# A three-part layer kernel whose first halves start from other counts and take their later loads piece by piece

## The reference

```python
x = x + attn_a(layernorm(x))   # delta-rule attention: per token S = a*S@(I - b k k^T) + b v k^T, o = (q@S)*gate, then @ Wo + bo
x = x + ffn(layernorm(x))      # silu(x @ gate^T) * (x @ up^T) @ down^T, int weights / 127
x = x + attn_b(layernorm(x))   # Mamba-like: causal convolution, chunked state space, gate, RMS norm, @ W_out
x = x + ffn(layernorm(x))
```

## Time and profile before

| | |
|---|---|
| median of three runs | 869.94 us (869.21 to 869.99) |
| profiled execution, first to last instruction (span) | 868.0 us |
| instructions | 16041 |
| TensorE busy | 769.9 us, 89% |
| VectorE (DVE) busy | 614.7 us, 71% |
| ScalarE (ACT) busy | 535.9 us, 62% |
| GpSimd (POOL) busy | 560.6 us, 65% |
| DMA | 22.16 MB, of it 11.59 MB read from HBM |

### The profile page before, as it was taken

How to read it: one execution, slowest core, us unless ns; L and a number is a source line. 1 busy time by engine, 2 the same in 40 slices (tenths; PEclk the granted TensorE clock), 3 DMA queues, 4 the chain that set the end, 5 groups by cost and what they waited for, 6 DMA issues and landing times. The chain is left out here.

```text
span 868.0 us, 16041 instructions
## 1 busy us (share of the span) xinstructions
PE 769.9 (89%) x5114; PEld 549.0 (63%) x5114; DVE 614.7 (71%) x1739; ACT 535.9 (62%) x1035; POOL 560.6 (65%) x917
## 2 busy tenths in 40 slices
PE   1469999999999896999848899999999999959997
PEld 1368888888888673666625466565555555646665
DVE  1356788788788544888673878988887776638885
ACT  2224443444454234899645888888887787818886
POOL 1276676677667512877711689779778876757785
PEclk9979999999999898999855999999999999979999
DMA  7511111211111100000000000000000000000112
GB/s 192 141 28 42 43 28 35 49 29 28 45 40 29 28 14 1 0 1 0 2 1 8 1 1 5 5 1 1 9 2 1 7 3 2 2 0 26 48 49 74
DMA packets 59420, 22.16 MB, mean 26 GB/s; under 512 B 22224, under 2 KB 59088, under 8 KB 59344
## 3 DMA queue, kind: packets, MB, share of 16 engines
q1 hardware_dynamic: 59344, 21.23, 9.6%
HBM read 11.59 MB, written 9.63 MB: 24 GB/s over the span
## 5 line engine op out<-in xcount | busy, mean ns | idle before, releaser
L1411 DVE SCALAR_TENSOR_TENSOR arena<-bank,convw_sb,arena 128x510 f32<-128x510 f32 (+2 forms) x192 | 142.5, 745 | 41.7 <-ACT arena L902 37.0
L671 POOL TENSOR_TENSOR arena<-arena 128x768 f32<-128x768 f32 x64 | 114.8, 1815 | 10.5 <-ACT arena L929 10.5
L645 POOL TENSOR_TENSOR arena<-ff,arena 128x512 f16<-128x512 f32 x64 | 73.6, 1159 | 23.2 <-ACT arena L871 21.2
L866 ACT ACTIVATE ff<-bank 128x512 f32<-128x512 f32 x96 | 56.2, 586 | 32.7 <-PE bank L1716 32.5
L578 POOL TENSOR_TENSOR leafV<-leafV,leaf_tmp 32x14 f32<-32x14 f32 (+6 forms) x224 | 62.1, 277 | 17.5
L1803 PE MATMUL bank<-xnT,win_sb 128*128 128x512 f32 x128 | 71.8, 644 | 0.0
L1227 DVE SCALAR_TENSOR_TENSOR ff<-bank,ff 128x512 f32<-128x512 f32 x96 | 64.7, 685 | 9.5 <-ACT ff L866 8.8
L759 ACT ACTIVATE xnT<-bank 128x512 f32<-128x512 f32 x34 | 20.3, 596 | 81.0 <-PE bank L1542 81.0
L767 ACT ACTIVATE xn<-x_all,shift,rstd 128x128 f32<-128x128 f32 x136 | 55.6, 481 | 23.7 <-DVE shift L1032 23.6
L774 ACT ACTIVATE ff<-bank 128x256 f32<-128x256 f32 (+2 forms) x80 | 33.9, 424 | 58.0 <-PE bank L1555 36.0
L923 ACT ACTIVATE arena<-bank 128x384 f32<-128x384 f32 x128 | 59.8, 491 | 13.8 <-PE bank L1818 13.6
(11 more groups left out here) (202 smaller groups left out, 2233.4 us busy)
## 6 DMA issues: line engine op xcount, KB each, us to landing
LT_dram<-arena SPq DMA_DIRECT2D x16, 256.0 KB, 2.3
ff<-R_dram SPq DMA_DIRECT2D x16, 256.0 KB, 2.8
out<-x_all SPq DMA_DIRECT2D x8, 512.0 KB, 3.2
x_all<-in_L_attn_a_x SPq DMA_DIRECT2D x7, 512.0 KB, 7.2
ff<-pieces_dram SPq DMA_DIRECT2D x48, 6.0 KB
x_all<-in_L_attn_a_x SPq DMA_DIRECT2D x2, 256.0 KB, 3.7
R_dram<-tab SPq DMA_DIRECT2D x2, 256.0 KB, 2.7
leafV<-LT_dram SPq DMA_DIRECT2D x16, 32.0 KB, 1.9
```

The source lines that it names most:

```text
L645: nc.gpsimd.tensor_tensor(of_block(hl[u], j), hidT[u][:, j, :], of_block(hh[u], j), ALU.subtract).then_inc(hl_done[u], 1)
L671: nc.gpsimd.tensor_tensor(score[h], cb[g % 2], hgam[h], ALU.mult).then_inc(score_done, 1)
L866: nc.scalar.activation(silu_g[u][:, j, :], bank[u][(1, 3, 1)[j]][:, :], ACT.Silu, scale=DEQUANT).then_inc(silu_done[u], 1)
L1411: nc.vector.scalar_tensor_tensor(acc_of[:, :, s:SEQ], src_of[:, :, 0:SEQ - s], convw_sb[:, r, TAPS - 1 - s:TAPS - s], acc_of[:, :, s:SEQ], ...
```

## The change

The counts begin at zero: `done(n)` is n + 1 (at least 0), `upto` is lower by 2, and the 84 increments of the paced semaphores are gone. The 18 increments by 1 stay. On SP only the first 512 KB load of x (groups 2 and 3) stays ahead of the zeroes; the other six and the 18 loads for the later phases are issued ahead of halves 1 to 8, each set behind the DMAs of the half before. The six share two semaphores instead of one: two loads are waited for in half 3, four in half 7. ACT's conversion of the feed-forward weights moves from half 3 to half 12. After the SP part the diff goes through POOL (`pool`), ACT (`act`), DVE (`dve`) and TensorE.

```diff
         def upto(n, u):
-            return STREAMS * n + u + 1
+            return STREAMS * (n - 1) + u + 1
...
         def done(n):
-            return n + STREAMS + 1
+            return max(n + 1, 0)
 
         def past(n):
-            return done(max(n, -1))
+            return done(n)
...
             sp.dma_start(tab[:, 2 * P:], tables[:, 2 * P:]).then_inc(tables_in, 16)
-            for k in range(1, PAIRS):
-                sp.dma_start(x_sb[:, k * step:(k + 1) * step, :],
-                             x_tok[:, k * step:(k + 1) * step, :]).then_inc(second_x_in if k == 1 else rest_x_in, 16)
...
+            def x_pair(k, loaded):
+                sp.dma_start(x_sb[:, k * step:(k + 1) * step, :], x_tok[:, k * step:(k + 1) * step, :]).then_inc(loaded, 16)
+
+            x_pair(1, second_x_in)
             sp.wait_ge(eye_in, 16)
             zeros = eye_zero[:, P:2 * P].unsqueeze(1).broadcast_to([P, GROUP_TILES, P])
             for scratch in R_dram:
                 sp.dma_start(dram_tiles(scratch), zeros).then_inc(diag_zeroed, 16)
             sp.wait_ge(diag_zeroed, 16 * STREAMS)
+
+            def later(h):
+
+                if h == 1:
+                    x_pair(2, third_x_in)
+                    x_pair(3, third_x_in)
+                if h in (2, 3):
+                    x_pair(2 * h, rest_x_in)
+                    x_pair(2 * h + 1, rest_x_in)
+                if h == 4:
+                    load(ff_int[:, 0, :].rearrange("p (k d) -> p k d", d=DIM), w_gate.rearrange("(k p) d -> p k d", p=P), later_in)
+                if h == 5:
+                    load(ff_int[:, 1, :].rearrange("p (k d) -> p k d", d=DIM), w_up.rearrange("(k p) d -> p k d", p=P), later_in)
+                    load(ff_int[:, 2, :], w_down, later_in)
+                if h == 6:
+                    load(win_sb[:, :], W_in, later_in)
+                    load(wout_raw[:, :, :], W_out.rearrange("(k p) d -> p k d", p=P), later_in)
+                    load(convw_sb[:, :, :], conv_w.rearrange("(k p) t -> p k t", p=P), later_in)
+                if h == 7:
+                    for k in range(CONV_BLOCKS):
+                        load(convb_sb[:, k:k + 1], column(conv_b[k * P:(k + 1) * P]), later_in)
+                    for k in range(INNER_BLOCKS):
+                        load(normw_col[:, k:k + 1], column(norm_w[k * P:(k + 1) * P]), later_in)
+                if h == 8:
+                    load(dtb_row[:, :], row(dt_bias), later_in)
+                    load(alog_row[:, :], row(A_log), later_in)
+                    for h in range(HEADS):
+                        half = (h % 2) * HEAD_DIM
+                        load(skip_col[half:half + HEAD_DIM, h // 2:h // 2 + 1],
+                             D_skip[h:h + 1].rearrange("(a n) -> a n", a=1).partition_broadcast(HEAD_DIM)[:, 0, :], later_in)
 
             def leaves_half(b, s, i, e, nxt):
...
-            in_order(leaves_half)
+            in_order(leaves_half, later)
...
-                    pool.wait_ge(rest_x_in, 16 * (PAIRS - 2))
+                    pool.wait_ge(third_x_in, 16 * 2)
+                if h == LAG_END + SETS:
+                    pool.wait_ge(rest_x_in, 16 * (PAIRS - 4))
...
-                if h == SETS - 1:
+                if h == GROUPS - SETS:
                     act.wait_ge(later_in, 16 * LATER_DMAS)
                     nc.scalar.activation(ff_raw[:, :, :], ff_int[:, :, :], ACT.Copy).then_inc(ff_float, 1)
...
                 if h == SETS - 1:
-                    dve.wait_ge(rest_x_in, 16 * (PAIRS - 2))
+                    dve.wait_ge(third_x_in, 16 * 2)
+                if h == 2 * SETS - 1:
+                    dve.wait_ge(rest_x_in, 16 * (PAIRS - 4))
...
-                        dve.wait_ge(down_mm, upto(i + PAIRS * run, u))
+                        dve.wait_ge(down_mm, max(upto(i + PAIRS * run, u), 0))
...
-            for s in paced:
-                pe.sem_inc(s, STREAMS)
             for s in (s for pair in per_stream for s in pair):
                 pe.sem_inc(s, 1)
```

More of the change, by code:

```diff
@@ L224, in build @@
         conv_bank, mid_bank, step_bank, y_bank = bank[0][0:2], bank[0][2:4], bank[1][0:2], bank[1][2:4]
-        group0_in, group1_in, second_x_in, rest_x_in, x_out = (
-            sem(n) for n in ("group0_in", "group1_in", "second_x_in", "rest_x_in", "x_out"))
+        group0_in, group1_in, second_x_in, third_x_in, rest_x_in, x_out = (
+            sem(n) for n in ("group0_in", "group1_in", "second_x_in", "third_x_in", "rest_x_in", "x_out"))
         eye_in, tables_in, k_in, attn_in, later_in = (sem(n) for n in ("eye_in", "tables_in", "k_in", "attn_in", "later_in"))
```

## The result

The changed kernel takes 859.47 us (median of 18 runs), the kernel before 870.4 us beside it. One of the 18, at 869.77 us and with the lowest granted clock, is a slow run; without it the median is 858.85 us (856.19 to 863.1). The ratio is 0.9865 (95% interval 0.9844 to 0.9885), so between 10.0 and 13.6 us are gained; 856.7 us had been forecast. In two later comparisons the changed kernel took 858.29 and 858.59 us, at ratios of 0.984 (0.980 to 0.988) and 0.986 (0.983 to 0.989). The profiled execution has a span of 859.7 us, only 8.3 us less than before.

What follows compares the result with a forecast made beforehand. Two late starts, TensorE's behind its increments and SP's behind its loads, were taken to bound the first 60 us; 8.3 + 4.9 = 13.2 us off the 869.94 us median gives 856.7 us, range 853.0 to 860.5 us.

Steps and rivals of the forecast that it cites:

- What bounds the beginning: First 60 us: TensorE starts late behind its increments, then SP issues LT's DMA late behind loads; POOL waits 14.6 us.
- The 84 increments: TensorE's start: without them, at 0.153 us each, the first transposes and LT of group 0 come 8.3 us earlier.
- SP's order: SP's queue before LT's first DMA: with fewer loads ahead, SP waits for LT and no longer the reverse; 4.9 us.
- They work only together: First DMA of LT: 13.2 us earlier needs both; either alone leaves LT at 31.11 us or its issue at 36.12.
- Half 1 moves whole: POOL still decides half 1, so `kinv` of group 1 moves the whole 13.2 us, from 42.36 to 29.2 us.
- The moved loads and the conversion: Halves 1 to 8: SP's issues hidden, read delay 0 (bound 4.4 us); ACT's conversion in half 12: zero.
- The sum: Whole kernel: 8.3 us from TensorE's start and 4.9 us from SP, 13.2 us gained, giving 856.7 us.
- More: Rival, chance 0.15: the shorter pause in half 1 leaves half 2 a high clock; 853 to 854.5 us.
- The signs of being wrong: Late transposes or LT DMA, DVE idle in halves 2 or 3, longer half 12, later phase over 2 us longer.
- Less, the loads disturb: Rival, chance 0.15: group 0's leaves and first two scratch reads 0.9 us late each, or zeroes late; 859.3 us.
- Only SP's part: Rival, chance 0.04: something else holds TensorE's first transposes, LT stays at 31.1 us, SP gains 5.0 us; 864.9 us.
- Slower, LT behind the loads: Rival, chance 0.04: halves 1 to 8, loads still in the rings delay LT's round trip; 22 us slower, 892 us.

Runs made afterwards that it cites:

- e2_order_only: The changed kernel with the old counts and the 84 increments put back, so only SP's new order stays; 864.71 us, ratio 0.9937 to the kernel before.
- e9_loads_ahead: The changed kernel with each half's later loads (halves 1 to 8) issued between the wait for LT and its DMA; 884.29 us, ratio 1.0154 to the kernel before.
- after_third: The changed kernel, unchanged, measured once more for its spread; 858.59 us (6 runs), its profiled execution 857.06 us.

## Why the prediction was right

**What bounds the beginning.** Right, by all the rows. TensorE's initial increments, at 0.153 us each and not at the 51 ns of their own duration, and SP's queue of loads were the two late starts, SP's the later one.

**The 84 increments: 8.3 us.** Measured 16.54 - 8.37 = 8.17 us, and 8.16 us at LT of group 0. The rest of the forecast of that step holds too: the group 1 statistics did not become the late part, though they began 0.6 us later than before and ended some 0.9 us ahead of the k product.

**SP's order: 4.9 us.** e2_order_only measured it alone as 4.9 us. The zeroes landed later than the 2.7 us I had added for them (median 7.2 us from issue), but still by about 18 us, so SP waited for LT.

**They work only together.** Right: 0 us from the counts, about 5 us from the order, 11 us or more from both.

**Half 1 moves whole.** Right: 13.07 us at `kinv`, 13.06 us at the second write of LT. One slip stands in the list of signs: behind the third write the next was to follow after 16.8 us; it followed after 15.45 us, as before (15.33). The sum does not use it.

**The moved loads and the conversion: nothing.** Nearly right. DVE waited 1.15 us for the first read from the scratch instead of 1.05, and halves 2 and 3 together gave back 0.2 us. The bound of 4.4 us was far too high for loads behind; for loads ahead e9_loads_ahead shows 3.2 us at the first write that they delay. The conversion ran from 210.09 us in half 12, and its half was not longer: the writes of LT on both sides stay 16.77 us apart (16.76 before).

**The sum: 13.2 us.** 13.2 us are there at 295 us in the first profiled execution, 12.5 in that of after_third. The measured 10.0 to 13.6 us contain the forecast, but the medians say less: 870.4 - 858.85 = 11.6 us, and 11.6 and 11.5 us in the two later comparisons. The term that was too small is the clock. I had allowed 1.5 us for it and looked for it in halves 1 and 2 only, as a gain. There it came out as before: the transposes of k take 1.11 us again and half 2 takes 17.64 us against 17.54, although the pause shrank from 8.6 to 3.7 us, so the rival *More* fell. It then cost 4.5 us at the end of the attention phase in two of three traced executions, and 3.1 us more near the end in one of them. That this is what the medians lack is likely from its size, but no run measures its share in them. Why the clock falls there in one execution and not in another was not found; the pauses ahead of it are the same.

**The signs of being wrong.** One of them came. A later phase was not to be longer than before by more than 2 us, and the stretch from the last read of the scratch to the first write of the pieces is longer by 4.5 us in the first profiled execution. The third one, with 146.1 us against 146.15 before, shows that the mechanism of the change need not bring it. The other signs did not come.

**The rivals.** *Less, the loads disturb* did not happen: the marks moved by 12.8 us and more. That its price, 859.3 us, is next to the measured 859.47 is chance. Its 1.8 us for loads issued in a crowd stood in no row; the traces of before and after now give 7.2 and 5.5 us, a difference of 1.7. *Only SP's part* is e2_order_only and not this change. *Slower, LT behind the loads* was the right mechanism at the right place with the right order of price (e9_loads_ahead: 14 us slower than before by the medians, where 22 were put down); its condition, loads still in the rings when LT is ready, is not met by the order chosen.

The Trainium skill (DMA: Bandwidth & Descriptors, Queues, rings and completion order) lets a completion land only behind every earlier write of the same DMA engine. e9_loads_ahead agrees, with 5.5 us instead of 2.3, but does not single this rule out: a write that merely queues behind the data of the loads would be late too.

## What to carry to other kernels

Start-up work that is late may be hidden by other start-up work that is later still: follow each engine's first real instruction back to what it waited for, and price such fixes together, since one alone can measure as zero. A queue that issues loads for much later needs only those ahead of its first urgent transfer; put the others directly behind an urgent transfer, never ahead of one. A shift made at the beginning arrives nearly whole through a steady pipeline (12.5 to 13.2 us at 295 us here). A gain of 1% has to be read at marks on the way, and in more than one trace, because the clock moves the end by several us from one execution to the next, and a mark by 1 or 2.

## What was unexpected

The semaphore increments follow each other every 0.153 us, three times their listed 51 ns. A load issued behind several others holds SP itself: up to 4 us for one of the seven issues before, 1.1 us for two in the changed kernel. And the granted clock differed between two executions of one program at the same place (0.61 and 0.85 over 18.7 us), while SP's writes of LT up to 71 us stood within 0.6 us of each other.
